# V projection spread over 29 of 32 attention steps, with two V buffers, in a one-layer attention and FFN kernel

## The reference, cut to what matters

```python
h = s4d_kernel(...)                       # (16, 128, 1024): 16 tiles of 128 tokens, D = 1024
x = layernorm(h)                          # kept transposed: features in partitions
q, k, v = x @ Wq.T + bq, x @ Wk.T + bk, x @ Wv.T + bv       # 32 heads of 32
p = softmax(causal(q @ k.T / sqrt(32)))   # within each tile of 128 tokens
h = h + (p @ v) @ Wo.T + bo               # h1
x2 = layernorm(h)
g, u = (x2 @ w(gate_q) + 0.02 * x2 @ A @ B for gate and up)  # 2752 hidden, 4-bit levels
h = h + (silu(g) * u) @ w(down_q) + 0.02 * (silu(g) * u) @ A @ B
```

## Time and profile before

| what | us |
|---|---|
| median of 3 runs (2087.77 to 2090.44) | 2087.96 |
| the profiled execution | 2088.66 |
| its span, first to last instruction | 2086.7 |
| PE busy | 1896.5 (91%) |
| DVE busy | 1163.6 (56%) |
| ACT busy | 612.7 (29%) |
| POOL busy | 618.0 (30%) |
| mean granted TensorE clock | 0.978 |

### The profile page before, as it was taken

One profiled execution on the slowest core, in us unless ns is written; L12 is line 12 of the kernel. 1 busy time (PEld: TensorE's weight loads), 2 busy tenths in 40 slices (PEclk: granted clock), 3 DMA queues, 4 the chain that ended last, 5 costly groups with the idle time before them and its releaser, 6 DMA issues.

```text
span 2086.7 us, 31307 instructions
## 1 busy us (share of the span) xinstructions
PE 1896.5 (91%) x13212; PEld 1029.0 (49%) x13212; DVE 1163.6 (56%) x1476; ACT 612.7 (29%) x869; POOL 618.0 (30%) x261
## 2 busy tenths in 40 slices
PE   0377699999999898878999999999999999999999
PEld 0367576666656554444554444444444444444444
DVE  8998547777777778855644544444444444210111
ACT  2154324334333334421112333333333333200000
POOL 2675013343333334433310322232232232011101
PEclk9998799999999999999999999999999999999999
DMA  2022211111132112135441321322322232533441
GB/s 90 10 71 60 65 35 33 39 39 35 29 94 72 27 36 60 57 104 194 154 147 61 119 94 62 101 91 61 101 91 77 85 101 72 195 120 116 142 142 41
DMA packets 99812, 173.32 MB, mean 83 GB/s; under 512 B 13984, under 2 KB 75168, under 8 KB 91744
## 3 DMA queue, kind: packets, MB, share of 16 engines
q1 hardware_dynamic: 99680, 171.41, 25.7%
HBM read 114.22 MB, written 56.11 MB: 82 GB/s over the span
## 4 chain that ended last, share of the span: by engine, by line
PE 73%; DVE 8%; POOL 2%; issue 2%; ACT 2%; DMA 1%; SPq 1%; ACTq 0%; DVEq 0%
PE acc L1194 14%; PE acc L1123 14%; PE acc L1124 14%; PE ps_p L930 3%; PE ps_p L931 3%; PE ps_p L932 3%; PE acc L1044 3%; PE acc L1045 3%; PE acc L1046 3%; PE ps_t L957 2%; PE ps_p L946 2%; PE ps_p L948 2%; PE ps_p L947 2%; DVE prob L1464 2%; PE ps_l L1139 2%
## 5 line engine op out<-in xcount | busy, mean ns | idle before, releaser
L1123 PE MATMUL acc<-x_hi,q_f 128*128 128x512 f16 x1376 | 522.0, 379 | 0.0
L1124 PE MATMUL acc<-x_lo,q_f 128*128 128x512 f16 x1376 | 521.5, 379 | 0.0
L1194 PE MATMUL acc<-down_levels,hid_parts 128*128 128x512 f16 x1376 | 300.1, 379 | 0.0
L890 POOL TENSOR_TENSOR prob<-prob,mx 128x1024 f32<-128x1024 f32 x64 | 121.4, 1897 | 421.9 <-DVE mx L1471 421.9
L1123 PEld LDWEIGHTS acc<-x_hi,q_f 128*128 128x128 f16 x1376 | 134.5, 98 | 174.8 <-issue 17.8
L899 POOL TENSOR_SCALAR q_f<-q_raw 128x2048 f16<-128x2048 int32 x22 | 121.1, 5504 | 316.3 <-PE acc L1124 315.4
L1194 PEld LDWEIGHTS acc<-down_levels,hid_parts 128*128 128x128 f16 x1376 | 133.2, 98 | 163.1 <-issue 5.0
L1124 PEld LDWEIGHTS acc<-x_lo,q_f 128*128 128x128 f16 x1376 | 134.7, 98 | 156.9
L930 PE MATMUL ps_p<-x_hi,w_qk 128*128 128x512 f16 x512 | 196.8, 384 | 0.0
L931 PE MATMUL ps_p<-x_lo,w_qk 128*128 128x512 f16 x512 | 196.0, 383 | 0.0
L932 PE MATMUL ps_p<-x_hi,w_qk 128*128 128x512 f16 x512 | 195.7, 382 | 0.0
(11 more groups left out here) (284 smaller groups left out, 3081.5 us busy)
## 6 DMA issues: line engine op xcount, KB each, us to landing
q_raw<-in_gu_q SPq DMA_DIRECT2D x22, 1024.0 KB, 7.1
hidden_parts<-hidden SPq DMA_DIRECT2D x42, 512.0 KB, 3.5
hid_parts<-hidden_parts SPq DMA_DIRECT2D x15, 1376.0 KB, 6.7
down_raw<-in_down_q SPq DMA_DIRECT2D x22, 512.0 KB, 5.1
w_raw<-in_w_qk SPq DMA_DIRECT2D x8, 1024.0 KB, 4.8
h_tokens<-n_tok SPq DMA_DIRECT2D x16, 512.0 KB, 3.8
o_parts<-ot SPq DMA_DIRECT2D x32, 256.0 KB, 2.3
wv_raw<-in_w_o SPq DMA_DIRECT2D x8, 1024.0 KB, 4.8
```

The costliest lines, as they stand in the source:

```text
L890: nc.gpsimd.tensor_tensor(prob[s % 2][p][:], prob[s % 2][p][:], bc(mx[p][:], H, 2), ALU.subtract).then_inc(s_sub[p], 1)
L1123: nc.tensor.matmul(acc[u % 2][:, m, :], lev, x2_hi[:, k, tok], start=(k == 0), stop=False)
L1124: last = nc.tensor.matmul(acc[u % 2][:, m, :], lev, x2_lo[:, k, tok], start=False, stop=(k == KT - 1))
L1194: last = nc.tensor.matmul(acc[n % 2][:, b, :], parts[n % 3][:, at], levels[:, i, b * CH:(b + 1) * CH], start=(i == 0 and part == 0), stop= ...
```

## The change

The V projection now has 3 pairs ahead of step 0 and one pair in each of the steps 0 to 28. V has two buffers; a pair's write waits for the values that read the same tiles two groups before, and `values(t)` waits only for the pairs of its own tiles. The V weights' maxima, scales and splits, the statistics, `output_scales` and the output weights lie in other steps, and on DVE they stand before `low_values` instead of behind it. SP exchanges the limits in the step of `output_scales`, loads the residuals in step 30 and the first three `o_parts` at the start of step 31, and `gu_scale` at the beginning. The square root `a_norm` moves into step 24. In the output stretch `factors()` is cut in two (the second part, from L1633 on, is `hidden_factors()`) and both stand later, as do A's low half, the b and down_a splits (n = 6, 10 and 8 on DVE; 5, 9 and 7 on ACT), b's second load (n = 7), `spread_low` (n = 7, 11, 15), and `low_rank`. ACT's stream in the output stretch follows the same order. `low(3)` stands behind `main(3, 1)`. Rooms: Wo's high part and `hidden` in v0, the b stack and `down_a` in v1.

The diff, cut to its core:

```diff
-V_STEPS = (VGROUPS - 1) * VPAIRS
+V_LEAD = 3
+V_STEPS = VGROUPS * VPAIRS - V_LEAD
...
-STAT_STEP = 14
-LIMIT_STEP = 21
-WO_STEP = 27
+STAT_STEPS = (16, 17, 18, 19, 21, 22)
+LIMIT_STEP = 23
+WO_STEP = 26
...
-    vh, vl = ([... for s in range(3)] ...)
+    vh, vl = ([... for s in two] ...)
...
+    def of_pair(q):
+        return q if q < V_LEAD else place(q - V_LEAD, 2)
... (SyncE)
         load_values(1)
         exchange(0)
         first.exchange(sp, 1)
         load(1)
-        load_values(2)
         sp.dma_start(bob[:], t["b_o"]).then_inc(s_bob, 16)
+        sp.dma_start(scl[:], t["gu_scale"]).then_inc(s_scl, 16)
         for s in range(STEPS):
+            if s == STEPS - 1:
+                sp.wait_ge(s_proj, place(V_STEPS - 1, 2) + 1)
+                for n in range(3):
+                    load_output(n)
             if s >= 2:
                 store(s - 2)
             if c == 0 and j + 1 < KT:
                 exchange(j + 1)
-            if n == 1 and g + 2 < VGROUPS:
-                first.exchange(sp, g + 2)
             if c == 3 and j + 2 < KT:
                 load(j + 2)
-            if n == 5 and g + 3 < VGROUPS:
-                load_values(g + 3)
-            if 0 <= s - STAT_STEP + 1 < 6:
-                load_job(s - STAT_STEP + 1)
-            if s == LIMIT_STEP - 1:
+            if s in (3, 8):
+                load_values(2 + s // 8)
+            if s in (4, 10):
+                first.exchange(sp, 2 + s // 10)
+            if s + 1 in STAT_STEPS:
+                load_job(STAT_STEPS.index(s + 1))
+            if s == LIMIT_STEP:
                 exchange_limits()
             if 0 <= s - WO_STEP + 1 < 4:
                 load_output_weights(s - WO_STEP + 1)
+            if s == STEPS - 2:
+                sp.wait_ge(s_wlo, 2 * KT)
+                load_residual(0)
+                load_residual(1)
+                sp.dma_start(araw[:], t["gu_a"]).then_inc(s_araw, 16)
... (TensorE)
-            pe.wait_ge(s_lo, VPAIRS if g == 0 else place((g - 1) * VPAIRS + VPAIRS - 1, 2) + 1)
+            pe.wait_ge(s_lo, of_pair(VPAIRS * g + 2 * (t % NCH) + 1) + 1)
...
-        for n in range(VPAIRS):
+        for n in range(V_LEAD):
             enter(n)
             value_tile(n, 0, 2 * n)
             value_tile(n, 0, 2 * n + 1)
...
-                g, n = s // VPAIRS + 1, s % VPAIRS
+                g, n = (s + V_LEAD) // VPAIRS, (s + V_LEAD) % VPAIRS
...
         for n in range(2, C):
             output(n, 0, 0, 4)
-            if n % 2 and n >= 3:
-                low_rank((n - 3) // 2)
-            if n == 2:
-                to_features(0)
+            if n in (2, 3):
+                to_features(n - 2)
+            if n % 2 == 0 and n >= 4:
+                low_rank(n // 2 - 2)
+            if n == C - 1:
+                low_rank(VPAIRS - 2)
             output(n, 0, 4, KT)
             output(n, 1, 0, 4)
-            to_features(n - 1)
+            if n >= 3:
+                to_features(n - 1)
             output(n, 1, 4, KT)
...
             main(u, 0)
-            low(u)
+            if u != 3:
+                low(u)
             if i < FULL:
                 main(u, 1)
+            if u == 3:
+                low(u)
... (ScalarE, in high_values; then in the steps)
-            if g >= 3:
-                act.wait_ge(s_val, (g - 2) * VPAIRS)
+            if g >= 2:
+                act.wait_ge(s_val, VPAIRS * (g - 2) + NCH + pair // 2 + 1)
...
+            if s in (1, 2):
+                first.high(nc, act, 1, s - 1)
+            if s in (6, 7):
+                first.high(nc, act, 2, s - 6)
+            if s in (13, 14):
+                act.wait_ge(s_proj, of_pair(2 * VPAIRS - 1) + 1)
+                first.high(nc, act, 3, s - 13)
+            if s == STAT_STEPS[0]:
                 squares()
+            if s == LIMIT_STEP + 1:
+                act.wait_ge(s_wscale, 1)
+                nc.scalar.activation(a_norm[:], lim[:, 0:1], ACT.Sqrt).then_inc(s_norm, 1)
             if 0 <= s - WO_STEP < 4:
                 high_output_weights(s - WO_STEP)
... (VectorE, the end of a step)
             if more and c == 0:
                 find_big(j + 1)
+            if s in (1, 6, 12):
+                first.find_scale(nc, dve, chain, 1 + s // 6)
+            if s in (4, 10):
+                first.find_big(nc, dve, chain, 2 + s // 10)
+            if s in (2, 3):
+                first.low(nc, dve, 1, s - 2)
+            if s in (7, 8):
+                first.low(nc, dve, 2, s - 7)
+            if s in (14, 15):
+                first.low(nc, dve, 3, s - 14)
+            if s in STAT_STEPS:
+                statistics(STAT_STEPS.index(s))
+            if s == LIMIT_STEP:
+                output_scales()
+            if 0 <= s - WO_STEP < 4:
+                low_output_weights(s - WO_STEP)
             if with_values(s):
-                low_values(place(s, 2), g + 1, n)
+                low_values(place(s, 2), (s + V_LEAD) // VPAIRS, (s + V_LEAD) % VPAIRS)
                 if s >= 1:
                     low_prob(s - 1, 2)
-            if 0 <= s - STAT_STEP < 6:
-                statistics(s - STAT_STEP)
-            if s == LIMIT_STEP:
-                output_scales()
-            if 0 <= s - WO_STEP < 4:
-                low_output_weights(s - WO_STEP)
... (VectorE, the output stretch)
         add_residual(0)
+        for a in four:
+            low_prob(STEPS - 1, a)
         low_output(STEPS - 1)
         normalise(0)
-        factors()
         add_residual(1)
-        dve.wait_ge(s_ahi, 1)
-        stt(ast[:, 1, ...], araw, ups[:, 0:1], ast[:, 0, ...], ...).then_inc(s_alo, 1)
-        normalise(1)
         low_features(0)
+        normalise(1)
         for n in range(2, C):
             ...
             low_features(n - 1)
             add_residual(n)
             normalise(n)
+            if n == 2:
+                factors()
+            if n == 3:
+                dve.wait_ge(s_ahi, 1)
+                stt(ast[:, 1, ...], araw, ups[:, 0:1], ast[:, 0, ...], ...).then_inc(s_alo, 1)
             if n == 4:
+                hidden_factors()
+            if n == 6:
                 low_b(0)
+            if n == 10:
+                low_b(1)
             if n == 8:
-                low_b(1)
-            if n == 6:
                 dve.wait_ge(s_adhi, 1)
                 ...
```

More of the change, by code:

```diff
@@ L587, in layer @@
     qh, ql, kh, kl = (put(n, [P, CH], F16, "qk", 1024 * i) for i, n in enumerate(("qh", "ql", "kh", "kl")))
-    vh, vl = ([put(f"{n}{s}", [P, C, VW], F16, f"v{s}", at) for s in range(3)] for n, at in (("vh", 0), ("vl", 8192)))
+    vh, vl = ([put(f"{n}{s}", [P, C, VW], F16, f"v{s}", at) for s in two] for n, at in (("vh", 0), ("vl", 8192)))
     prob = [[put(f"prob{s}{p}", [P, 2 * BPC, H], F32, "prob", 4096 * (2 * s + p)) for p in two] for s in two]
@@ L619, in layer @@
     lsb = [put(f"low_term{s}", [P, 2, CH], F32, "probt", 4096 * s) for s in two]
-    bst = put("gu_b_stack", [P, 2, I], F16, "v0")
-    a_d = put("down_a", [P, IT, 2 * R], F16, "v0", 4 * I)
-    scl = put("gu_scale", [P, 2, IT], F32, "v0", 4 * I + 4 * IT * R)
+    bst = put("gu_b_stack", [P, 2, I], F16, "v1")
+    a_d = put("down_a", [P, IT, 2 * R], F16, "v1", 4 * I)
+    scl = small("gu_scale", [P, 2, IT])
     ad_raw = put("down_a_raw", [P, IT, R], F32, "ot")
@@ L625, in layer @@
     q16 = [put(f"q_f16{s}", [P, 2, D], F16, "w", 8192 + 4096 * s) for s in two]
-    hid = [put(f"hidden{s}", [P, C, 2, H], F16, "v1", 8192 * s) for s in two]
+    hid = [put(f"hidden{s}", [P, C, 2, H], F16, "v0", 8192 * s) for s in two]
     levels = put("down_levels", [P, IT, D], F16, "wv")
@@ L971, in values @@
                         r = slice(HD * a, HD * a + HD)
-                        last = nc.tensor.matmul(ps_o[r, q], of_v[g % 3][:, tile, col + HD * a:col + HD * a + HD],
+                        last = nc.tensor.matmul(ps_o[r, q], of_v[g % 2][:, tile, col + HD * a:col + HD * a + HD],
                                                 of_p[a][:, q],
@@ L1276, in _ @@
         high_weights(0, 1)
-        for n in range(2, VPAIRS):
-            high_values(n, 0, n)
-            if n == 3:
-                first.high(nc, act, 1, 0)
-            if n == 4:
-                first.high(nc, act, 1, 1)
+        high_values(2, 0, 2)
         for s in range(STEPS):
-            j, c, g, n, mixed = s // NCH, s % NCH, s // VPAIRS, s % VPAIRS, s <= V_STEPS
+            j, c, mixed = s // NCH, s % NCH, s <= V_STEPS
             if s >= 2:
@@ L1511, in low_output_weights @@
         def low_output_weights(g):
-            dve.wait_ge(s_val, 3 * VPAIRS)
             for k in two:
@@ L1526, in _ @@
         low_weights(0, 1)
-        first.find_scale(nc, dve, chain, 1)
-        for n in range(2, VPAIRS):
-            low_values(n, 0, n)
-            if n in (4, 5):
-                first.low(nc, dve, 1, n - 4)
+        low_values(2, 0, 2)
         for s in range(STEPS):
-            j, c, g, n, mixed = s // NCH, s % NCH, s // VPAIRS, s % VPAIRS, s <= V_STEPS
```

(4 more changed lines are left out.)

107 lines of the change are left out of this document (48 added, 59 removed).

## The result

The changed kernel takes **2070.58 us** (median of 4 runs, 2068.10 to 2074.96), the one before 2087.86 beside it (2087.72 to 2090.44, 4 runs): a ratio of 0.9917, 95% interval 0.9898 to 0.9935. Forecast were 2069, and 2059 to 2079.

What follows compares the result with a forecast made beforehand. TensorE was taken as busiest, its idle stretches as the gain: loop -3.3 (excess 43.9 to 40.6), first loads -9.2, output stretch -5.1, low(3) -1.6, sum -19.2 from 2088.66; less 0.7 for the median, 2069 us, range 2059 to 2079.

Steps and rivals of the forecast that it cites:

- Parts 1 and 2: Score loop: moving V costs 0; DVE work of length E ahead of V's split adds E - 2.0, sum 10.2 us.
- Part 3: Step 23: limits behind load(7) arrive late, DVE waits; excess 11.5 us, lower bound 9.8 if the write lands in 4.0.
- Part 4: Steps 26 to 29: DVE's output weights wait for ACT and delay V's split; 18.9 us, clock falls included.
- Part 5: Step 24: the moved square root needs two ACT table loads, 1.28 us each; taken as 0, at most 1.3.
- Part 6: Last scores to last values: early o_parts loads remove the 9.2 us wait, two smaller waits follow; 37.6 becomes 28.4, -9.2.
- Part 7: Output stretch: moving factors() removes the 7.9 us wait and some low clock, smaller waits follow; 10.4 becomes 5.3, -5.1.
- part 8: Early FFN: low(3) behind main(3,1) covers PE's wait for low_stack; -1.6 us.
- Rival (b): Output stretch keeps its stall: the queue behind gu_b delays later o_parts or residual by 7.9 us; 2076, chance 0.12.
- signs: Among them: 30.7 us after step 23's scores, DVE waiting 9 there; 24 to 25 us after steps 26 and 27.
- rival (a): Step 23: the limits are in time, so it costs only 1.8 to 2.5 us; 9 us less, 2060, chance 0.09.
- (c): Steps 23 to 29: after the stalls PE stays at 1.2 GHz; +20 to +24 us, 2091, chance 0.04.
- Rival (d): Steps 24 to 28: filling with V gives nothing, already in the forecast; if it worked, 2053, chance 0.02.

Runs made afterwards that it cites:

- Run 1: The changed kernel with SP exchanging the limits one step earlier, ahead of the weight tile: 2060.3 us.
- Run 6: The changed kernel with the output projection's first loads (residuals, feature weights, three partial outputs) issued after SP's loop, as before the change: 2077.6 us.
- run 9: The changed kernel with SP issuing the first tile's store, third residual and fourth partial outputs ahead of the last step's store and next weights: 2065.5 us.
- Runs 3 to 5: Run 3, run 5 and, between them, the changed kernel with DVE's statistics, output scales and output weights' split back behind low_values and low_prob: 2078.0 us.
- Run 3: The changed kernel with limits exchanged one step earlier and ACT's conversion of the output weights first in its step: 2050.0 us.
- run 5: The kernel before with only DVE's statistics, output scales and weights' split moved ahead of low_values, V in its old steps: 2076.0 us.
- Run 11: As run 10, but with the old order of the output stretch on PE, ACT and DVE: 2053.2 us.
- run 10: Run 3 and run 9 together, plus low_prob(31, 0) ahead of add_residual(0) and A's low half one place earlier on DVE: 2040.8 us.
- run 7: The changed kernel with the output stretch in its old order on PE, ACT, DVE and SP, early first loads kept: 2066.5 us.
- run 2: The changed kernel with ACT's conversion of the output weights ahead of its conversions of V and the probabilities: 2057.7 us.

## Why the prediction was right or wrong

**Parts 1 and 2, V moved and DVE's extra work: right.** Part 1 said 0. The stretch from the first V matmul to the first scores lost five pairs and became 25.8 us shorter (60.2 to 34.4); five steps became V steps, each 5.2 us longer at least, 26.2 in all. So the move costs 0.3 to 0.4 and no more, and clean V steps still take 19.2: the second buffer's wait costs nothing. For E - 2.0 ahead of V's split, 3.0, 1.6, 0.6, 1.7 and 1.2 were forecast for steps 4, 8, 10, 12 and 16; measured over 19.21 were 2.96, 1.57, 0.56, 1.64 and 1.16, and 0.17 for each statistics step (0.2). Sum 9.3 against 10.2; 0.5 of the difference is the clock fall that did not follow. (The minimum of 441.0 in the prediction goes with 19.21 a step; with its 19.2 it would be 440.8.)

**Part 3, the limits: right in its mechanism, 1.7 too high.** The write landed after 5.2 us (4.85 + 0.35 forecast). The broadcast took 3.4, not the 5.4 of the earlier trace rows, so the limits were there at scores + 5.6 instead of + 7.3. Excess 9.8 instead of 11.5. That is the number of the lower bound, but not its case: the write was not faster, the broadcast was. Why it took 3.4 here and 5.4 before is open.

**Part 4, the output weights: the mis-sized term of the loop.** The delays themselves were right: 5.0 and 4.0 forecast, 4.96 and 3.92 measured. The 1.1 us added to each for the clock was not there. Run 1 shows why no such sum may be made: its step 27 takes 23.13 us with no low clock, the changed kernel's takes 23.13 with 3.41 us of it. Run 1's step 27 (windows view):

```profile
806.49:829.62 23.13, 19.61 (x211) 12.25 (x211) 15.18 (x18) 8.90 (x13) 7.54 (x4) 1.00 0.18 58
```

The chain through DVE and POOL sets the length there, and slower matmuls fit below it: where they run at full clock, PE waits another 0.9 us for a `ptl` later in the step. With step 29 (1.6 instead of 2.4) part 4 was 15.9, not 18.9; that the clock cost nothing is 2.2 of these 3.0. Excess after: 9.3 + 9.8 + 15.9 = 35.0 instead of 40.6; from 43.9 that is -8.9, and -8.4 was measured; most of the rest is the 0.3 to 0.4 of the move.

**Part 5, the square root: right.** ACT's timeline in step 24 has both table loads, the next instruction 0.01 us behind the first:

```profile
750.30 1.28 ACT L1331 ACT_TABLE_LOAD   x1
751.59 0.20 ACT L1331 ACTIVATE a_norm<-limit 128x1 f32<-128x1 f32 x1
...
754.16 1.28 ACT L1260 ACT_TABLE_LOAD   x1
```

The step takes 19.59, the 0.4 of its maximum and nothing for the loads.

**Part 6, the first loads: right.** The stretch from the last scores to the last values was to become 28.4 and became 29.3, so 8.3 us less instead of 9.2; both successors came, 0.93 for the forecast 0.9 and 1.65 for 1.2. Run 6 finds 10.6, because in the new order the old loads make that stretch 39.9, 2.3 longer than in the kernel before.

**Part 7, the output stretch: this step failed.** It said that `factors()` leaves the way of `add_residual(1)`, so that the 7.9 goes with 2.45 of low clock, and 1.8, 2.5 and 1.0 come back: -5.1. From the start of the last values to the end the tail lost 2.4 us, of which part 8 has 1.6, so part 7 gave **0.8**. The 7.9 did go. Three gaps came for it, 6.6 us: 2.3 for tile 3's `o_parts` (1.8 forecast), 3.0 for A's low half (2.5) and one that I had not counted, 1.3 before tile 2's features. The term for the clock was wrong as well: instead of 1.45 less, 0.5 more came (4.9 us of work at half clock there before, 5.9 after).

The third gap comes from the new order itself and not from the queue. DVE's timeline of the changed kernel, and POOL's residual of tile 2:

```profile
934.06 1.22 DVE L1631 TENSOR_TENSOR x_lo<-pn,x_hi 128x1024 f16<-128x1024 f32 x1 [9.63 <-ACT x_hi L1350]
935.20 1.27 DVE L1616 SCALAR_TENSOR_TENSOR h_tok<-acc,wo_back,residual 128x1024 f32<-128x1024 f32 x1
928.12 2.34 POOL L911 TENSOR_TENSOR residual<-residual,bo_rows 128x1024 f32<-128x1024 f32 x1 [23.30 <-DMA residual<-h_tokens]
```

The residual is there at 930.46, but `add_residual(2)` stands behind `low_features(1)`, which waits for PE's transposes of tile 1, now half a tile later. In run 9 the same residual is there 19 us earlier (from the last scores), and the 1.3 stays. Rival (b), a stall that the queue behind `gu_b` keeps, is thus true of 2.3 us alone, the gap that run 9 takes away.

**Part 8: right** in the wait; its 1.6 is about what the clock does to the same stretch from run to run.

So two errors of about 5 us, the loop 5.1 too pessimistic and the tail 5.2 too optimistic, cancelled in the sum: that 2069 came so near 2070.6 was luck. Of the signs that it named, three came smaller: step 23 29.0 instead of 30.7, DVE's wait there 7.2 instead of 9, step 27 23.1 instead of 24 or more. Neither rival (a), a limit in time, nor (c), a clock that stays low, came. Rival (d) asked what filling the late steps with V is worth. Runs 3 to 5 answer it: with the two new waits in place it costs 5.0 us (647.62 against 642.67 with the order alone); without them it gives 14.9 (627.77 against 642.67). Run 3 also has ACT's edit, which was not tried without the spread; in run 5's four steps with output weights DVE waits only 1.0 us in all for ACT's `wo_hi`, so that little of the 14.9 can be its.

**The tail in one rule.** Its length follows from the gaps and from half of the low-clock time in which PE has work: less both, the tails of all thirteen traces are 1167.8 to 1168.3. There are 11.3 us of gaps in the changed kernel and 5.9 us of work at half clock, 9.1 and 3.4 in run 9: 2.3 + 1.3 = 3.6 from that, 3.7 measured. Run 11 against run 10: 14.6 - 5.6 = 9.0 of gaps and 5.3 / 2 = 2.6 of clock are 11.6, as measured.

## What to carry to other kernels

- When a job is moved ahead of a critical instruction in its queue, ask of **every input** of that job who makes it and in what place of *that* queue. Here the change was right in its order and lost 20 us to two inputs, one DMA behind a 1 MB load and one ACT conversion behind work that was not missed when it came later; each cost one moved call to mend.
- A large wait that is removed from a stretch with several late inputs may break up into small ones: before booking the gain, list the successors one by one until one has slack. An edit that measures as zero, as the reorder here, may be worth something once the others are made (6.2 us with the transfers early).
- A fall of the clock costs where TensorE itself sets the length. In a step whose chain runs through other engines it cost nothing here (23.13 us with and without), and it must not simply be added to the delay. Step 28 took 18.19 with it and 17.50 without (run 1), but step 29 behind it 15.60 and 16.17.

## What the runs showed of the hardware

**A VectorE instruction can wait for GpSimd without any semaphore.** In run 11 DVE's timeline has two operations on a few numbers that take 2.02 and 5.35 us:

```profile
900.75 0.18 DVE L559 RECIPROCAL g_up<-g_pow 128x4 f32<-128x4 f32 x1
900.96 2.02 DVE L560 TENSOR_SCALAR g_up<-g_up 128x4 f32<-128x4 f32 x1
...
903.08 5.35 DVE L1644 TENSOR_SCALAR g_b_back<-g_pow 128x2 f32<-128x2 f32 x1
```

The same two take 0.17 and 0.22 in run 7. POOL's timeline at that time:

```profile
900.61 2.35 POOL L914 TENSOR_TENSOR residual<-residual,bo_rows 128x1024 f32<-128x1024 f32 x1 [11.99 <-DMA residual<-h_tokens]
903.05 5.37 POOL L909 TENSOR_SCALAR q_f<-q_raw 128x2048 f16<-128x2048 int32 x1
```

DVE's two end at 902.98 and 908.43, POOL's at 902.96 and 908.42: each stood until POOL's instruction was done. That is 7.0 us on the path of tile 1, less 3.7 for which run 7 waits for its scales there, so 3.3 net: PE's wait is 11.5 instead of 8.2. It is most of what run 11 cost above its expectation, and no wait of the profile names it. It was the earlier transfer that set it off: with the residual there sooner, POOL's two instructions fall on DVE's chain. It is no accident of one run. In the first stage of the kernel before, one instruction of DVE comes 16 times (L422):

```profile
104.07 1.58 DVE L422 SCALAR_TENSOR_TENSOR n_rs<-n_mv,n_rs 128x1 f32<-128x1 f32 x1
103.71 1.92 POOL L211 TENSOR_TENSOR phase<-a,c_re 128x1024 f32<-128x1024 f32 x1
```

Twelve times it starts during an instruction of POOL, takes 0.49 to 1.58 us and ends 0.01 to 0.02 us behind POOL's; the other four times it takes 0.16. Run 10 pays as well: its first `h_nrm` (128 x 1024) takes 1.99 instead of 0.81 during POOL's `q_f`, and PE's wait for it is 2.9 instead of the 1.7 of run 9. Reciprocals are not held: the one above went through in 0.18, and all 38 of the kernel before that start during an instruction of POOL take 0.21 or less. The Trainium skill ("Advanced Engine Details and Errata", VectorE Performance Modes) says that GpSimd and VectorE's two-port modes share a port and block each other; the long ones here fit it. What the modes ask of each operand was not tried.

**A small transfer landed about when the one ahead of it did**: the same 5 KB took 1.4 us with nothing just ahead (run 1), 4.0 behind 128 KB that took 4.0 (the kernel before), and 5.2 behind 1 MB that took 5.4 (the changed kernel).

**The clock's falls are not the same from run to run** even where the work is: behind step 27's gap, 2.1 us in both, it fell for 3.41 us in the changed kernel and not at all in run 1; behind step 26's (3.14 us) it fell in both and not in runs 6 and 9, and behind step 23's wait of 7.3 us for 6.83 in one and 10.24 in another (run 2).
